# Cross-attention layer with experts: heads weighed by 64-column matmuls, one reciprocal and one product a unit, and the norm of some slots moved to ScalarE

## Chip, core and metric

One core of one Trainium2 chip runs the whole layer in one launch. The metric is the device time in microseconds, the median of several runs.

## The reference, cut to what matters

There are 64 sequences of 64 tokens with 128 features, 16 heads of 8 features, and 8 experts of which each token uses two.

```python
def _attn(q_in, k_in, v_in, wq, bq, wk, bk, wv, bv, wo, bo, causal):
    Q = (q_in @ wq + bq).reshape(Bq, Sq, H, HD)
    Kp = (k_in @ wk + bk).reshape(Bq, Sk, H, HD)
    V = (v_in @ wv + bv).reshape(Bq, Sk, H, HD)
    scores = jnp.einsum('bqhd,bkhd->bhqk', Q, Kp) / jnp.sqrt(jnp.float32(HD))
    if causal:
        scores = jnp.where(mask, scores, -jnp.inf)
    a = jax.nn.softmax(scores, axis=-1)
    o = jnp.einsum('bhqk,bkhd->bqhd', a, V).reshape(Bq, Sq, Dm)
    return o @ wo + bo
...
x = _layernorm(x + _attn(x, x, x, ..., causal=True), ln1_g, ln1_b)
x = _layernorm(x + _attn(x, ctx, ctx, ..., causal=False), ln2_g, ln2_b)
x = _layernorm(x + _moe(x, ...), ln3_g, ln3_b)
```

## The kernel before

The 4096 tokens are 32 tiles of 128 rows, each tile two sequences of 64 tokens. A unit is one attention (self or cross) over one tile, so there are 64 units; two units with consecutive tiles make a block. The program of each engine is written out as a loop over slots. Slot g starts unit g: self blocks first, then two self units and two cross units in turn, then only cross units; the 64 units fill slots 0 to 63. A unit passes through the engines over several slots: scores and maxima in slot g, transposed scores and exponentials in g + 1, weighing and the division by the sum in g + 2, turning the outputs, the output projection, the residual and its statistics in g + 3, the norm and its gain in g + 4, turning the normed rows in g + 5. The projections for later blocks are prepared in the same slots (`prepared`, `crossed`). From slot 33 on, each slot also holds one or more tiles of the experts (88 tiles in all, most of them after the attention), and slots 24 to 26, 40 to 42 and 56 to 58 hold routing steps. Each engine executes its instructions in order and waits on counting semaphores; the order within a slot is that of the functions `slot(g)`.

In a slot, TensorE does, in order: turn outputs and normed rows (`turn_both`; after the scores where `turns_late(g)` holds, that is in slots without tiles before slot 33), transposed scores of unit g - 1 (`scores_T`, which needs VectorE's `max_diag`), scores of unit g (`scores`), an expert tile's first products, router logits, `weigh` of unit g - 2, `out_proj` of unit g - 3, the tile's second products, and projections for later blocks. VectorE does: low parts of the projections (`low_parts`), `norm` of unit g - 4, `maxima` of unit g, the low parts of the first 10 heads' probabilities, logits, `outputs` of unit g - 2 and `residual` of unit g - 3, then routing and sums. ScalarE does the two exponentials of unit g - 1 (full and high half), copies of what TensorE turned, the tile's copies and Gelu, and the high parts of projections. GpSimd does `gain` of unit g - 4 (waits for the norm), scatters of routed rows, the low parts of the other six heads, `spread` of unit g - 3 (the reciprocal root, from VectorE's mean and variance) and the low part of the second norm's output.

`weigh` multiplies the probabilities of a pair of heads (keys on the partitions) with the values in fp16, as three products of high and low parts. Two sequences share a tile. Both halves of the columns, one for each head of the pair, meet values of both heads, so half of the 36 columns of each result are not used: the rows of head h need only the columns of head h. The values hold an extra column of ones per head, whose result is the softmax's denominator. `outputs` divides by it, for each half of the partitions apart, into `o_n`, whose other half was set to zero at the start, so that `turn_o` can sum it over 128 partitions.

Of the kernel before, what the change touches and what calls it, by code (L numbers as in the profile page):

```python
# [7 lines left out]
HD = D // H  # L8
P = 128
# [7 lines left out]
HP = H // 2  # L17
# [367 lines left out]
def build(nc, x, ctx_in, cst, w, out):  # L385
# [17 lines left out]
    with st:  # L403
# [52 lines left out]
        o_n = [sb(f"o_n{p}", [P, 2, 2, HP, HD]) for p in range(2)]  # L456
# [5 lines left out]
        rstd = [sb(f"rstd{p}", [P, 1]) for p in range(2)]  # L462
        carrier = sb("carrier", [P, 1])
# [42 lines left out]
        LG_COL = 36 * HP  # L506
# [66 lines left out]
        zeroed, ZEROED = sem("constants_set"), 22  # L573
# [248 lines left out]
        def _(pool):  # L822
# [6 lines left out]
            for p in range(2):  # L829
                pool.memset(o_n[p][:, :, :, :, :], 0.0).then_inc(zeroed, 1)  # L830
# [4 lines left out]
            pool.wait_ge(zeroed, 14)  # L835
            for a in range(2):
                for p in range(2):
                    for b in range(2):
                        pool.memset(v_hi[a][p][64 * b:64 * b + 64, :, b, :, HD:HD + 1], 1.0).then_inc(zeroed, 1)
                        pool.wait_ge(zeroed, 14 + 4 * a + 2 * p + b + 1)  # L840
# [28 lines left out]
            def spread(u):  # L869

                a, n = u.kind, u.buf
                pool.wait_ge(mv_done[a], u.count())
                pool.tensor_tensor(veps[n][:, :], mv[n][:, 1:2], eps[:, 0:1], ALU.add).then_inc(ve_done[a], 1)  # L873
                pool.wait_ge(ve_done[a], u.count())
                pool.tensor_tensor(rstd[n][:, :], veps[n][:, :], minus_half[:, 0:1], ALU.pow).then_inc(rs_done[a], 1)  # L875

# [57 lines left out]
            def slot(g):  # L934
# [17 lines left out]
                if u := unit_at(g - 3):  # L952
                    spread(u)
# [13 lines left out]
        def _(act):  # L967
# [72 lines left out]

            def x2_high(u):

                act.wait_ge(x_done[CROSS], u.count())
                act.activation(x2_hl[:, u.tile(), 0:D], x_rows[:, u.tile(), :], ACT.Copy).then_inc(x2_hi_ready, 1)
# [48 lines left out]
            def slot(g):  # L1093
# [71 lines left out]
        def _(dve):  # L1165
# [52 lines left out]

            def outputs(u):

                a = u.kind
                dve.wait_ge(pv_ready[a], u.count())
                o = bank[:, O_B, 0:HP * 36].rearrange("p (a b c d) -> p a b c d", a=HP, b=2, c=2)
# [11 lines left out]
            def residual(u):  # L1235
# [10 lines left out]
                dve.wait_ge(res_done[a], u.count())  # L1246
                dve.bn_stats(stats[n][:, :], res[n][:, :]).then_inc(st_done[a], 1)
                dve.wait_ge(st_done[a], u.count())
                dve.tensor_copy(carrier[:, :], consts[:, 0:1])
                dve.bn_aggr(mv[n][:, :], stats[n][:, :]).then_inc(mv_done[a], 1)  # L1250

            def norm(u, v):

                a, n = u.kind, u.buf
                dve.wait_ge(rs_done[a], u.count())
# [202 lines left out]
            def slot(g):  # L1458
# [20 lines left out]
                if u := unit_at(g - 4):  # L1479
                    norm(u, same_buffers(g - 4))  # L1480
# [50 lines left out]
        def _(pe):  # L1531
# [125 lines left out]
            def weigh(u):  # L1657
# [5 lines left out]
                a2, p2 = home(a, b)  # L1663
                for p in range(HP):
                    ph, pl = [v[u.buf][:, 2 * p:2 * p + 2, :].rearrange("p h q -> p (h q)") for v in (p_hi, p_lo)]
                    vh, vl = [v[a2][p2][:, u.pair, :, 2 * p:2 * p + 2, :].rearrange("p b h d -> p b (h d)")
                              for v in (v_hi, v_lo)]
# [266 lines left out]
```

## Time and profile before

| | us |
|---|---|
| median of 3 runs | 741.23 (740.14 to 742.75) |
| profiled execution | 739.34 |
| span of the profiled execution | 737.5 |
| busy in the span: TensorE, weight loads | 566.0, 451.3 |
| busy in the span: VectorE, ScalarE, GpSimd | 493.5, 436.8, 360.7 |

The profile is one execution. The span runs from the first to the last instruction; what lies between span and time is start and end of the launch. Matmuls are pipelined and their ends are modelled, so the starts of consecutive matmuls say more than their durations. In the names of engines PE is TensorE, PEld its weight loads, DVE VectorE, ACT ScalarE, POOL GpSimd. Idle time in square brackets stands before an instruction, with what ended it.

### The profile page before, as it was taken

What the parts mean: (1) busy time and instruction counts of PE and PEld (TensorE: products, weight loads), DVE (VectorE), ACT (ScalarE), POOL (GpSimd) and SP (SyncE); (2) the same over time, 40 slices, a digit from 0 to 9 for tenths busy, and PEclk for the clock granted to TensorE, in tenths of its full rate; (3) what the DMA queues carried; (4) which work ended last, traced back from release to release, by engine and by line L of the source; (5) the groups of instructions that cost most, each with busy time, mean ns of one, the idle gap of its engine ahead of it and who ended that gap; (6) DMA issues with size and microseconds to landing.
All of it is one profiled execution on the core that took longest, in us unless ns stands there. A gap on an engine that the chain in (4) does not pass through costs nothing. (4 is left out here: it accounts for less than half of the span.)

```text
span 737.5 us, 21262 instructions
## 1 busy us (share of the span) xinstructions
PE 566.0 (77%) x7870; PEld 451.3 (61%) x7870; DVE 493.5 (67%) x1345; ACT 436.8 (59%) x814; POOL 360.7 (49%) x564
## 2 busy tenths in 40 slices
PE   2579767877857779887798888857788877788980
PEld 1256545655544557766677666646687877677980
DVE  4388999999997877778777679996632424231163
ACT  1244665555534459997699789956666763444320
POOL 8133435345327734543576356728852574540360
PEclk9997999799987789999899999997999999999995
DMA  4455434645543456454555746434358898898730
GB/s 101 133 175 158 135 108 148 174 150 164 172 125 94 126 162 205 133 162 133 153 175 153 219 151 195 145 97 143 126 164 255 266 292 287 270 282 257 237 105 28
DMA packets 142837, 124.65 MB, mean 169 GB/s; under 512 B 12752, under 2 KB 125152, under 8 KB 142736
## 3 DMA queue, kind: packets, MB, share of 16 engines
q1 hardware_dynamic: 135024, 113.06, 50.5%
q0 software_dynamic: 4176, 8.53, 4.1%
q10 hardware_dynamic: 3536, 1.70, 0.8%
q8 instruction: 64, 1.05, 0.6%
q14 instruction: 37, 0.30, 0.1%
HBM read 86.81 MB, written 38.54 MB: 170 GB/s over the span
## 5 line engine op out<-in xcount | busy, mean ns | idle before, releaser
L1212 DVE TENSOR_REDUCE row_max<-bank 128x16 bf16<-128x1024 f32 x64 | 78.1, 1221 | 32.3 <-PE bank L1627 31.2
L1767 PE MATMUL bank<-w_in,w_hl 128*128 128x128 f32 x704 | 98.8, 284 | 0.0
L1004 ACT ACTIVATE probT<-bank 128x1024 f32<-128x1024 f32 x64 | 65.6, 1024 | 51.2 <-PE bank L1652 50.2
L887 POOL TENSOR_TENSOR prob_lo<-probT,prob_hi 128x384 f16<-128x384 f32 x64 | 66.8, 1044 | 46.9 <-ACT prob_hi L1007 46.5
L1767 PEld LDWEIGHTS bank<-w_in,w_hl 128*128 128x128 f32 x704 | 86.5, 194 | 0.2
L873 POOL TENSOR_TENSOR veps<-mv,eps 128x1 f32<-128x1 f32 x64 | 16.0, 251 | 136.8 <-DVE mv L1250 136.8
L1056 ACT ACTIVATE w_hl<-bank 128x512 f32<-128x512 f32 x88 | 52.6, 598 | 43.5 <-PE bank L1753 42.9
L896 POOL DMA_INDIRECT xs<-x_hl,pos x60 | 63.6, 1060 | 22.8 <-issue 17.2
L1753 PE MATMUL bank<-xT,w_in 128*128 128x128 f16 x1056 | 74.2, 220 | 0.0
L912 POOL DMA_INDIRECT w_hl<-ys,pos x52 | 51.7, 994 | 41.0 <-DMA ys<-w_hl 26.8
L1677 PE MATMUL bank<-consts,o_n 128*128 128x64 f32 x256 | 44.6, 300 | 30.4 <-DVE o_n L1231 26.8
L1640 PE MATMUL bank<-max_diag,consts_bf 128*128 128x512 bf16 x128 | 44.7, 434 | 28.7 <-DVE max_diag L1217 28.6
L1007 ACT ACTIVATE prob_hi<-bank 128x1024 f16<-128x1024 f32 x64 | 65.1, 1018 | 0.0
L1753 PEld LDWEIGHTS bank<-xT,w_in 128*128 128x128 f16 x1056 | 63.8, 99 | 0.0
L1677 PEld LDWEIGHTS bank<-consts,o_n 128*128 128x128 f32 x256 | 36.2, 204 | 44.8 <-issue 30.4
L1652 PEld LDWEIGHTS bank<-q_st,k_all 128*64 128x64 f16 x2048 | 41.9, 121 | 32.5 <-issue 32.5
L1217 DVE TENSOR_TENSOR max_diag<-consts_bf,row_max 128x1024 bf16<-128x1024 bf16 x64 | 59.9, 936 | 2.2
L1205 DVE TENSOR_TENSOR prob_lo<-probT,prob_hi 128x640 f16<-128x640 f32 x64 | 58.3, 910 | 4.0 <-ACT prob_hi L1007 3.9
L861 POOL TENSOR_TENSOR yg<-yn,ln_g 128x128 f32<-128x128 f32 x64 | 29.6, 462 | 56.1 <-DVE yn L1259 56.1
L1749 PE MATMUL bank<-chosen_biases,b_all 128*128 128x128 f16 x352 | 35.1, 222 | 23.0 <-ACT xT L1049 15.0
L1259 DVE TENSOR_SCALAR yn<-res,mv,rstd 128x128 f32<-128x128 f32 x64 | 25.7, 401 | 37.4 <-POOL rstd L875 36.5
L1652 PE MATMUL bank<-q_st,k_all 128*64 128x64 f16 x2048 | 49.3, 207 | 0.0
(182 smaller groups left out, 1536.6 us busy)
## 6 DMA issues: line engine op xcount, KB each, us to landing
w_in<-w_scr SPq DMA_DIRECT2D x96, 512.0 KB, 4.6
q_scr<-q_hl SPq DMA_DIRECT2D x64, 128.0 KB, 2.7
k_scr<-k_hl SPq DMA_DIRECT2D x64, 128.0 KB, 2.3
q_st<-q_scr SPq DMA_DIRECT2D x32, 256.0 KB, 3.1
k_all<-k_scr SPq DMA_DIRECT2D x128, 64.0 KB, 2.5
xs_tile<-xs SPq DMA_DIRECT2D x42, 128.0 KB
ys<-w_hl SPq DMA_DIRECT2D x42, 128.0 KB
xs<-xs_tile SPq DMA_DIRECT2D x19, 256.0 KB, 3.3
```

The source lines that it names most:

```text
L887: pool.tensor_tensor(p_lo[u.buf][:, h, :], probT[u.buf][:, h, :], p_hi[u.buf][:, h, :], ALU.subtract).then_inc(lo_second[u.kind], 1)
L896: pool.indirect_dma_start(xs[c], bass.IndirectOffsetOnAxis(pos[c][:, k, t:t + 1], 0), x2_hl[:, n, :], None).then_inc(scattered[c], 16)
L1004: act.activation(probT[u.buf][:, :, :].rearrange("p h q -> p (h q)"), bank[:, KEYS:KEYS + 2, :].rearrange("p a n -> p (a n)"), ACT.Exp, sc ...
L1007: act.activation(p_hi[u.buf][:, :, :].rearrange("p h q -> p (h q)"), bank[:, KEYS:KEYS + 2, :].rearrange("p a n -> p (a n)"), ACT.Exp, sca ...
L1056: act.activation(hid[x.par][:, :, :].rearrange("p c t -> p (c t)"), expert_h(x), ACT.Gelu, scale=1 / W1_SCALE).then_inc(h_done, 1)
L1205: dve.tensor_tensor(p_lo[u.buf][:, h, :], probT[u.buf][:, h, :], p_hi[u.buf][:, h, :], ALU.subtract).then_inc(lo_first[u.kind], 1)
L1212: dve.reduce_max(row_max[u.buf][:, :], bank[:, SC:SC + 2, :].rearrange("p a (h k) -> p (a h) k", k=S), AX.X).then_inc(max_done[a], 1)
L1217: dve.tensor_tensor(max_diag[u.buf][:, :, :, :], dl, m, ALU.mult).then_inc(diag_ready[a], 1)
L1652: last = pe.matmul(bank[64 * h:64 * h + 64, KEYS + n, 64 * hh:64 * hh + 64], k[:, gg, j, c:c + 64], q[:, gg, c:c + 64], start=False, stop= ...
L1677: last = pe.matmul(turned_o[:, 64 * b:64 * b + 64], o_n[u.buf][:, b, :, :, :].rearrange("p c a d -> p (c a d)"), consts[:, C_DELTA:C_TRI], ...
L1753: last = pe.matmul(v[:, c * P:(c + 1) * P], w1_t[x.wb][:, i, c * P:(c + 1) * P], xT[x.par][:, j * P:(j + 1) * P], start=False, stop=True, ...
L1767: last = pe.matmul(expert_y(x), hid[x.par][:, c, :], w2_t[x.wb][:, c, :], start=False, stop=c == FC - 1, skip_group_check=True)
```

## The change

`weigh` uses each head's probabilities as weights of 64 columns and streams that head's 18 columns of values (both sequences, ones included); the two heads of a pair write to the two halves of the partitions. There are 48 matmuls a unit where there were 24. All 18 columns of each result are used, so `outputs` becomes one reciprocal and one product over 128 partitions, `o_n` has half the size and needs no zeros, and `turn_o` takes four 64 x 64 products for two of 128 x 64. On VectorE the order of a slot's end is now: residual of unit g - 3, reciprocal of unit g - 2, statistics of g - 3, product of g - 2 (in place of a small copy), mean and variance of g - 3. GpSimd makes an offset, -mean x rstd, after the root; both `norm`s wait for it. In slots where `turns_late(g)` holds, ScalarE does the norm of unit g - 4 from scale and offset, behind its copies of the turned rows; elsewhere VectorE does it as before.

```diff
-        o_n = [sb(f"o_n{p}", [P, 2, 2, HP, HD]) for p in range(2)]
+        o_n = [sb(f"o_n{p}", [P, 2, HP, HD]) for p in range(2)]
+        shift = [sb(f"shift{p}", [P, 1]) for p in range(2)]
-        LG_COL = 36 * HP
+        LG_COL = 2 * (HD + 1) * HP
 # GpSimd, start
-            for p in range(2):
-                pool.memset(o_n[p][:, :, :, :, :], 0.0).then_inc(zeroed, 1)
 # GpSimd
-            def spread(u):
+            def spread(u, v):
                 a, n = u.kind, u.buf
                 pool.wait_ge(mv_done[a], u.count())
+                if v:
+                    pool.wait_ge(yn_ready[v.kind], v.count())
                 pool.tensor_tensor(veps[n][:, :], mv[n][:, 1:2], eps[:, 0:1], ALU.add).then_inc(ve_done[a], 1)
                 pool.wait_ge(ve_done[a], u.count())
                 pool.tensor_tensor(rstd[n][:, :], veps[n][:, :], minus_half[:, 0:1], ALU.pow).then_inc(rs_done[a], 1)
+                pool.wait_ge(rs_done[a], 2 * u.count() - 1)
+                pool.tensor_scalar(shift[n][:, :], mv[n][:, 0:1], rstd[n][:, :], -1.0, ALU.mult, ALU.mult).then_inc(rs_done[a], 1)
 # ScalarE
+            def norm(u, v):
+                a, n = u.kind, u.buf
+                act.wait_ge(rs_done[a], 2 * u.count())
+                if u.count() > 1:
+                    act.wait_ge(yn_ready[a], u.count() - 1)
+                if v:
+                    act.wait_ge(yT_ready[v.kind], v.count())
+                    act.wait_ge(yg_done[v.kind], v.count())
+                act.activation(yn[n][:, :], res[n][:, :], ACT.Identity, bias=shift[n][:, :], scale=rstd[n][:, :]).then_inc(yn_ready[a], 1)
...
                 if turns_late(g):
                     both_turned(g)
+                    if u := unit_at(g - 4):
+                        norm(u, same_buffers(g - 4))
 # VectorE
-            def outputs(u):
+            def denominators(u):
                 a = u.kind
                 dve.wait_ge(pv_ready[a], u.count())
-                for h in range(2):
-                    r = slice(64 * h, 64 * h + 64)
-                    last = dve.reciprocal(rden[u.buf][r, :, :], o[r, :, :, h, HD])
-                last.then_inc(rden_done[a], 1)
+                dve.reciprocal(rden[u.buf][:, :, :], weighed()[:, :, :, HD]).then_inc(rden_done[a], 1)
+            def outputs(u):
+                a = u.kind
                 dve.wait_ge(rden_done[a], u.count())
-                for h in range(2):
-                    r = slice(64 * h, 64 * h + 64)
-                    last = dve.tensor_tensor(o_n[u.buf][r, :, h, :, :].rearrange("p b a d -> p a b d"), o[r, :, :, h, 0:HD],
-                                             rden[u.buf][r, :, :].unsqueeze(3).to_broadcast([64, HP, 2, HD]), ALU.mult)
-                last.then_inc(on_ready[a], 1)
+                dve.tensor_tensor(o_n[u.buf][:, :, :, :].rearrange("p b a d -> p a b d"), weighed()[:, :, :, 0:HD],
+                                  rden[u.buf][:, :, :].unsqueeze(3).to_broadcast([P, HP, 2, HD]), ALU.mult).then_inc(on_ready[a], 1)
...
+                if v:
+                    dve.wait_ge(yn_ready[v.kind], v.count())      # in residual(u, v)
...
-                if u := unit_at(g - 4):
+                if (u := unit_at(g - 4)) and not turns_late(g):
                     norm(u, same_buffers(g - 4))
...
-                if u := unit_at(g - 2):
-                    outputs(u)
-                if u := unit_at(g - 3):
-                    residual(u)
+                u, v = unit_at(g - 3), unit_at(g - 2)
+                if u:
+                    residual(u, same_buffers(g - 3))
+                if v:
+                    denominators(v)
+                if u:
+                    row_stats(u)
+                    mean_and_variance(u, v)      # outputs(v) before the aggregate
+                elif v:
+                    outputs(v)
 # TensorE
+                n = 2 * (HD + 1)
                 for p in range(HP):
-                    for k, (pt, v) in enumerate(((ph, vh), (ph, vl), (pl, vh))):
-                        last = pe.matmul(bank[:, O_B, 36 * p:36 * p + 36], pt, v, start=k == 0, stop=k == 2,
-                                         skip_group_check=True)
+                    for k, (pt, v) in enumerate(((p_hi, v_hi), (p_hi, v_lo), (p_lo, v_hi))):
+                        for h in range(2):
+                            last = pe.matmul(bank[64 * h:64 * h + 64, O_B, n * p:n * p + n], pt[u.buf][:, 2 * p + h, :],
+                                             v[a2][p2][:, u.pair, :, 2 * p + h, :], start=k == 0, stop=k == 2,
+                                             skip_group_check=True)
...
                 for b in range(2):
-                    last = pe.matmul(turned_o[:, 64 * b:64 * b + 64],
-                                     o_n[u.buf][:, b, :, :, :].rearrange("p c a d -> p (c a d)"),
-                                     consts[:, C_DELTA:C_TRI], start=True, stop=True)
+                    for h in range(2):
+                        r = slice(64 * h, 64 * h + 64)
+                        last = pe.matmul(turned_o[r, 64 * b:64 * b + 64], o_n[u.buf][r, b, :, :].rearrange("p a d -> p (a d)"),
+                                         consts[r, C_DELTA:C_TRI], start=True, stop=True)
```

## Rows read from the trace of the kernel before

**Rows 1.** Windows: stretch, length, PE, PEld, DVE, ACT, POOL busy, clock, DMA share, GB/s.

```profile
45.00:255.00 210.00, 161.95 (x2321) 112.41 (x2321) 186.75 (x457) 107.26 (x207) 97.97 (x169) 0.87 0.49 146
255.00:530.00 275.00, 226.94 (x3446) 179.93 (x3445) 212.26 (x573) 225.66 (x381) 151.44 (x235) 0.93 0.52 158
```

**Rows 2.** VectorE's groups by form, 45 to 255 us: count, busy, mean ns, idle before.

```profile
L1212 DVE TENSOR_REDUCE row_max<-bank 128x16 bf16<-128x1024 f32 x29 | 35.4, 1219 | 2.8 <-PE bank L1627 2.4
...
L1231 DVE TENSOR_TENSOR o_n<-bank,rden 64x128 f32<-64x128 f32 x57 | 16.5, 289 | 1.4
L1226 DVE RECIPROCAL rden<-bank 64x16 f32<-64x16 f32 x56 | 14.0, 250 | 0.4
...
L1259 DVE TENSOR_SCALAR yn<-res,mv,rstd 128x128 f32<-128x128 f32 x28 | 11.2, 399 | 13.1 <-POOL rstd L875 12.7
...
L1476 DVE SCALAR_TENSOR_TENSOR w_hl<-w_in,w_hl 128x512 f16<-128x512 f32 x8 | 5.3, 665 | 0.0
```

**Rows 3.** TensorE's timeline over four slots: start, duration, line, tiles, count, idle before.

```profile
170.64 0.62 PE L1640 MATMUL bank<-max_diag,consts_bf 128*128 128x512 bf16 x2 [0.84 <-DVE max_diag L1217]
...
177.30 0.62 PE L1640 MATMUL bank<-max_diag,consts_bf 128*128 128x512 bf16 x2 [1.40 <-DVE max_diag L1217]
...
181.18 0.49 PE L1685 MATMUL bank<-wo,oT 128*128 128x128 f32 x2 [0.46 <-ACT oT L1016]
...
181.94 0.61 PE L1607 MATMUL bank<-wv,inT 128*128 128x128 f32 x4
183.50 0.62 PE L1640 MATMUL bank<-max_diag,consts_bf 128*128 128x512 bf16 x2 [0.95 <-DVE max_diag L1217]
...
186.10 0.63 PE L1677 MATMUL bank<-consts,o_n 128*128 128x64 f32 x4 [0.92 <-DVE o_n L1231]
...
187.66 0.36 PE L1704 MATMUL bank<-rw,x_tile 128*128 128x8 f32 x2 [0.81 <-ACT x_tile L1030]
...
189.96 1.06 PE L1607 MATMUL bank<-wv,inT 128*128 128x128 f32 x4
...
197.74 0.62 PE L1640 MATMUL bank<-max_diag,consts_bf 128*128 128x512 bf16 x2 [0.87 <-DVE max_diag L1217]
```

**Rows 4.** TensorE's timeline inside two slots, the parts that are priced.

```profile
173.96 0.18 PE L1669 MATMUL bank<-v_hi,prob_hi 128*128 128x36 f16 x1
...
174.56 0.47 PE L1685 MATMUL bank<-wo,oT 128*128 128x128 f32 x2
...
177.76 0.59 PE L1645 MATMUL bank<-consts_bf 128*128 128x512 bf16 x2
178.28 0.69 PE L1652 MATMUL bank<-q_st,k_all 128*64 128x64 f16 x32
178.81 0.61 PE L1627 MATMUL bank<-k_all,q_st 128*64 128x256 f16 x8
179.34 0.66 PE L1677 MATMUL bank<-consts,o_n 128*128 128x64 f32 x4
179.84 0.28 PE L1690 MATMUL bank<-consts,yn 128*128 128x128 f32 x1
```

**Rows 5.** ScalarE's groups by form, the whole span.

```profile
L1025 ACT ACTIVATE x1T<-bank,ln_bc,ln_gc 128x128 f32<-128x128 f32 x32 | 14.8, 463 | 0.0
```

**Rows 6.** GpSimd's groups by form, 45 to 255 us.

```profile
L896 POOL DMA_INDIRECT xs<-x_hl,pos x12 | 13.5, 1124 | 3.6 <-issue 3.6
...
L873 POOL TENSOR_TENSOR veps<-mv,eps 128x1 f32<-128x1 f32 x28 | 8.8, 314 | 80.1 <-DVE mv L1250 80.1
```

**Rows 7.** TensorE's timeline in a slot with scatters.

```profile
245.00 0.18 PE L1669 MATMUL bank<-v_hi,prob_hi 128*128 128x36 f16 x1 [1.78 <-POOL prob_lo L887]
```

**Rows 8.** Waits from 255 to 530 us: total, times, longest.

```profile
DVE row_max L1212 <- PE bank L1627: 24.9, 14, 4.6
...
ACT oT L1016 <- PE bank L1690: 19.3, 14, 3.1
```

**Rows 9.** GpSimd's timeline at the start.

```profile
8.35 0.60 POOL L830 MEMSET o_n<- 128x256 f32 x2
```

More of the change, by code:

```diff
@@ L572, in build @@
         cbf_ready = sem("consts_bf16_ready")
-        zeroed, ZEROED = sem("constants_set"), 22
+        zeroed, ZEROED = sem("constants_set"), 20
         b1_bo_ready = sem("ln1_b_plus_ca_bo")
@@ L834, in _ @@
             pool.memset(b_all[:, :], 0.0).then_inc(zeroed, 1)
-            pool.wait_ge(zeroed, 14)
+            pool.wait_ge(zeroed, 12)
             for a in range(2):
@@ L839, in _ @@
                         pool.memset(v_hi[a][p][64 * b:64 * b + 64, :, b, :, HD:HD + 1], 1.0).then_inc(zeroed, 1)
-                        pool.wait_ge(zeroed, 14 + 4 * a + 2 * p + b + 1)
+                        pool.wait_ge(zeroed, 12 + 4 * a + 2 * p + b + 1)
             for dst, src in [(v[:, :], w[name].partition_broadcast(P)) for v, name in (
@@ L952, in slot @@
                 if u := unit_at(g - 3):
-                    spread(u)
+                    spread(u, same_buffers(g - 3))
                 if (u := unit_at(g - 6)) and u.kind == CROSS:
@@ L1217, in maxima, with weighed, residual @@
                 dve.tensor_tensor(max_diag[u.buf][:, :, :, :], dl, m, ALU.mult).then_inc(diag_ready[a], 1)
+            def weighed():
+                return bank[:, O_B, 0:LG_COL].rearrange("p (a b d) -> p a b d", a=HP, b=2)
+            def denominators(u):
+                a = u.kind
+                dve.wait_ge(pv_ready[a], u.count())
+                dve.reciprocal(rden[u.buf][:, :, :], weighed()[:, :, :, HD]).then_inc(rden_done[a], 1)
             def outputs(u):
                 a = u.kind
-                dve.wait_ge(pv_ready[a], u.count())
-                o = bank[:, O_B, 0:HP * 36].rearrange("p (a b c d) -> p a b c d", a=HP, b=2, c=2)
-                for h in range(2):
-                    r = slice(64 * h, 64 * h + 64)
-                    last = dve.reciprocal(rden[u.buf][r, :, :], o[r, :, :, h, HD])
-                last.then_inc(rden_done[a], 1)
-                dve.wait_ge(rden_done[a], u.count())
-                for h in range(2):
-                    r = slice(64 * h, 64 * h + 64)
-                    last = dve.tensor_tensor(o_n[u.buf][r, :, h, :, :].rearrange("p b a d -> p a b d"), o[r, :, :, h, 0:HD],
-                                             rden[u.buf][r, :, :].unsqueeze(3).to_broadcast([64, HP, 2, HD]), ALU.mult)
-                last.then_inc(on_ready[a], 1)
-            def residual(u):
+                dve.wait_ge(rden_done[a], u.count())
+                dve.tensor_tensor(o_n[u.buf][:, :, :, :].rearrange("p b a d -> p a b d"), weighed()[:, :, :, 0:HD],
+                                  rden[u.buf][:, :, :].unsqueeze(3).to_broadcast([P, HP, 2, HD]), ALU.mult).then_inc(on_ready[a], 1)
+            def residual(u, v):
                 a, n = u.kind, u.buf
                 dve.wait_ge(wo_ready[a], u.count())
+                if v:
+                    dve.wait_ge(yn_ready[v.kind], v.count())
                 if a == SELF:
@@ L1245, in residual, with row_stats, mean_and_variance @@
                 dve.tensor_tensor(res[n][:, :], bank[:, O_B, WO_COL:WO_COL + D], r, ALU.add).then_inc(res_done[a], 1)
[L1246 to L1250, printed above, removed]
+            def row_stats(u):
+                dve.wait_ge(res_done[u.kind], u.count())
+                dve.bn_stats(stats[u.buf][:, :], res[u.buf][:, :]).then_inc(st_done[u.kind], 1)
+            def mean_and_variance(u, v):
+                dve.wait_ge(st_done[u.kind], u.count())
+                if v:
+                    outputs(v)
+                else:
+                    dve.tensor_copy(carrier[:, :], consts[:, 0:1])
+                dve.bn_aggr(mv[u.buf][:, :], stats[u.buf][:, :]).then_inc(mv_done[u.kind], 1)
             def norm(u, v):
                 a, n = u.kind, u.buf
-                dve.wait_ge(rs_done[a], u.count())
+                dve.wait_ge(rs_done[a], 2 * u.count())
+                if u.count() > 1:
+                    dve.wait_ge(yn_ready[a], u.count() - 1)
                 if v:
@@ L1491, in slot @@
                     logits(u)
-                if u := unit_at(g - 2):
-                    outputs(u)
-                if u := unit_at(g - 3):
-                    residual(u)
+                u, v = unit_at(g - 3), unit_at(g - 2)
+                if u:
+                    residual(u, same_buffers(g - 3))
+                if v:
+                    denominators(v)
[3 more added lines that the diff above has]
+                elif v:
+                    outputs(v)
                 if (c := routed_at(g, 2)) is not None:
```

3 lines of the change are left out of this document (removed).

## The prediction

> **What bounds the kernel now.** I read the windows first [rows 1]. From 45 to 255 us the kernel runs the slots that have attention but no expert tiles. VectorE is busy 186.75 of 210 us there, TensorE (modelled, overlapping) 161.95, ScalarE 107.26, GpSimd 97.97. From 255 to 530 us, where every slot also has expert tiles, TensorE (226.94 of 275) and ScalarE (225.66) lead and VectorE has 212.26. After 530 us only tiles and the last expert pass remain; the chain that ended last lies in that part and is TensorE's, so what is gained or lost before 530 us shifts it as a whole.
>
> Then VectorE's groups of the first stretch [rows 2]: 29 maxima, so 29 slots. Outside its own work VectorE sat idle mainly before the norm: 13.1 us, 12.7 of it until GpSimd's rstd came. Then TensorE's order over four slots [rows 3], 170.64 to 197.74 us, the repeating pattern: two self units, two cross units, 27.10 us, 6.78 a slot. Each slot begins with the product that needs VectorE's max_diag, and TensorE waited 1.40, 0.95 and 0.87 us for it in three of the four, and 0.92 us for o_n in one. So VectorE sets the pace there, with TensorE and ScalarE close behind. That closeness decides the forecast.
>
> **VectorE, slots without tiles.** Removed a slot: the norm, 0.40 us, and the wait before it, 12.7 / 28 = 0.45 us [rows 2]; one reciprocal of two (0.25) and one product of two (0.29), because the new ones cover 128 partitions with as many elements per partition (16 and 128) as each half had [rows 2]. A one-element copy goes too; it overlaps and I count nothing. Sum 1.39 us a slot, which would leave 5.39. The new order, residual, reciprocal, statistics, product, aggregate, has the product waiting on a reciprocal with another instruction between, so nothing is queued behind a fresh dependence. The heads' product is the fourth instruction after the start, as before, so on_ready does not come earlier; the aggregate has four instructions in front of it instead of seven, so it comes 0.54 us earlier.
>
> **TensorE, every unit.** Weighing: 24 matmuls of 36 columns take 174.56 - 173.96 = 0.60 us, 25 ns each [rows 4]. The new 48 have 64-column weights and 18 columns to stream. The nearest row is the scores' transposed product, also 64-column weights alternating between the two partition halves: 32 in 178.81 - 178.28 = 0.53 us, 16.6 ns each [rows 4]. 48 x 16.6 = 0.80 us. Entering such weights costs something: 178.28 - 177.76 = 0.52 us for two products of 512 columns, whose repeat without a change of shape (177.30 to 177.76, two) took 0.46 [rows 3, 4]; 0.06 in, and I take as much out. The weighing thus rises by 0.80 + 0.12 - 0.60 = 0.32 us. Lower bound 0 (half the columns per weight load, so half the time for each), upper bound 48 x 25 ns + 0.12 - 0.60 = +0.72.
>
> Turning the outputs: two fp32 products (four records) take 179.84 - 179.34 = 0.50 us [rows 4]; four of 64 x 64 take eight records. No row shows fp32 on a quarter of the array. Lower bound -0.10 (the halves overlap wholly), upper bound 8 x 0.125 + 0.1 = 1.1, so +0.60. I take +0.15, nearer the low end, because the 16.6 ns row shows the two halves overlapping.
>
> The page TensorEngine Tiling (Array Packing) of the Trainium skill, section Instruction Overhead, says each matmul has about 60 cycles of overhead however few columns it streams, and its section Key Properties says that a change of tiling mode drains the engine. Counted per instruction the first would make 48 matmuls 1.2 us; the row of 16.6 ns speaks against that for alternating halves, and the 0.06 us agrees with a small drain. By that page the weighing would rise 0.60 us, 0.28 more than I take, and over the 15 steady slots of the sum below 4.2 us of gain would go: 727 instead of 723.
>
> **What becomes the bound there.** TensorE's period without its waits for max_diag is 27.10 - 1.40 - 0.95 - 0.87 = 23.88 us. I leave the 0.92 us for o_n in: later in that slot TensorE waits 0.81 us for ScalarE's x_tile anyway [rows 3]. Added: weighing 0.32 in each of three slots, turn 0.15 in one; in the second slot both together are 0.47, which the 0.46 us wait for oT [rows 3] hides; in the last two the turn hides in the x_tile wait. 3 x 0.32 + 0.15 = 1.11, so 24.99. In one slot the four products of V took 1.06 us against 0.61 for the same in the slot before [rows 3], and the granted clock over the stretch was 0.87 [rows 1]: TensorE had waited for o_n and x_tile, then ran for a while at the lower of its two levels (1.2 and 2.4 GHz). Those products lost 0.45; with the projections beside them I estimate 1.0 us for the slot, and with fewer waits I give back half, 0.5. Period 24.5, 6.12 a slot: 0.66 gained, out of VectorE's 1.39.
>
> **ScalarE and GpSimd.** ScalarE's norm is the form of its y copy, 128 x 128 with a scale and an offset per row: 0.46 us [rows 5]. It stands behind two exps and both turned copies. ScalarE is busy half of this stretch [rows 1], so 29 x 0.46 fits, but the norm is in order: behind it wait the copies of projections, then the next exps. It needs rstd and the offset one slot after the aggregate, and the aggregate now comes earlier. GpSimd's offset is one 128 x 1 operation that multiplies twice: between the add beside it, 0.31 us [rows 6], and two of them, 0.62; I take 0.31, and either is hidden under its 80.1 us of waiting for mv in this stretch [rows 6]. What moves for GpSimd is its gain: it waits for ScalarE's norm, late in the slot, and the low parts of the probabilities are queued behind the gain. The weighing that needs them is a slot later, so about 1 us of room; free. In slots with tiles VectorE's norm waits for the offset too, +0.31, against an aggregate 0.54 earlier: nothing.
>
> The four slots with scatters (twelve of 1.12 us [rows 6]) are GpSimd's already: TensorE waited 1.78 us for its low parts [rows 7]. No gain there.
>
> **Slots with tiles.** Here VectorE loses 0.54 us a slot, but it is not the pace: it waits 24.9 us for scores, and ScalarE waits 19.3 us in 14 slots for the turned y, right behind the turned outputs [rows 8]. 14 x 0.15 = 2.1 us lost. Four slots hold VectorE's routing steps and gain 0.54 each, 2.2. The weighing's 0.32 stands ahead of the down products, which wait for ScalarE's tile copies often enough that I take it as hidden; exposed in half of 32 slots it costs 5.1 us. Net 0.
>
> **Start.** Two memsets of o_n go, 8.35 us, 0.60 for both [rows 9], ahead of GpSimd's loads: 0.5 us.
>
> **Sum.** 29 slots: 4 with scatters 0; 8 where VectorE also splits W1 (0.67 each, [rows 2]) and 2 with routing, where more of the 1.39 is usable: 1.0 each, 10.0; the other 15 at 0.66, 9.9. Less 0.1 in each of 25 slots, because in slots that split projections VectorE itself will be late for the scores: 2.5. 10.0 + 9.9 - 2.5 + 0.5 = 17.9. From the profiled execution's 739.34 us: 721.4. The median of the runs shown, 741.23, is 1.9 above; so 723.
>
> **Rivals.** *VectorE stays the pace*: TensorE overlaps the halves wholly and its clock rises with fewer waits. Then 25 slots gain 1.39: 34.8 us, 706. For it: VectorE's 89% busy. Against: 23.88 of 27.10.
>
> *TensorE too slow*: the small matmuls cost 25 ns each, as the row of the old weighing has it, and the eight records do not overlap: +0.72 + 0.60 = 1.32 a unit. A steady slot becomes 23.88 / 4 + 1.32 = 7.29, 0.51 slower than now; 15 slots give 8 us, the 14 waits for the turn 8 more, and the ten others nothing: slower, about 757. It decides from 6.78 - 5.97 = 0.81 us a unit on. Against: the 16.6 ns row. The page's overhead of the Trainium skill named above is this rival's first half.
>
> *GpSimd and ScalarE in line*: the gain behind ScalarE's norm pushes the low parts beyond the weighing, as GpSimd already does in the scatter slots [rows 7]. At 0.35 us a slot over 25 slots half the gain goes: 732. Against: about 1 us of room.
>
> *Nothing*: ScalarE's order alone (exps, copies, norm, projections) fills 6.78 us a slot: 741. Against: it is half idle.
>
> **Chances.** Forecast 0.55, VectorE the pace 0.15, GpSimd in line 0.15, nothing 0.05, TensorE too slow 0.10. The forecast by itself runs from 715 (full 1.39 in the ten slots, VectorE never late, clock all given back) to 730 (weighing exposed in half the tile slots, no clock back). The range reaches to 706 and, past 732, to 739. About 0.3%, 2.2 us, is what a measurement can tell from no change. Faster 0.82, same 0.06, slower 0.12.
>
> **What would show it.** Right: plain slots without tiles near 6.1 us; VectorE's wait for rstd gone and its waits for the scores grown; TensorE's waits for max_diag small; weighing near 0.92 us, the turn near 0.65; slots with scatters and with tiles as they are. Wrong: the weighing waiting for GpSimd's low parts in plain slots; the turned outputs over 1.0 us; TensorE's clock in the first stretch lower than 0.87; tile slots longer than now.

## The result, and the profile after

The kernel after takes 722.4 us (median of four runs, 720.5 to 724.3) against 741.4 for the kernel before on the same chip: a ratio of 0.974 with a 95% interval from 0.971 to 0.978. Medians here are over all runs of a kernel, and ratios leave out the runs of a slower state that some executions fall into. The forecast was 723. The profiled execution took 722.76 us with a span of 720.9. The total came out as predicted; its parts did not, as the slots show. I cut both traces, one execution of each kernel, at the starts of the 64 maxima, one a slot:

| stretch | before, us | after, us | gained | by the prediction's terms |
|---|---|---|---|---|
| up to the maxima of slot 3 | 46.11 | 46.58 | -0.5 | 0.5 |
| slots 3 to 14, no router logits yet | 88.12 | 72.83 | 15.3 | 9.4 |
| slots 15 to 23, router logits in five of the nine | 61.00 | 61.02 | 0.0 | 5.0 |
| slots 24 to 32, scatters and routing among them | 75.40 | 73.52 | 1.9 | 2.9 |
| slots 33 to 60, with tiles | 242.28 | 240.12 | 2.2 | 0 |
| the rest of the span | 224.59 | 226.83 | -2.2 | 0 |

The column of the prediction's terms takes 0.9 for each of the 8 slots that split W1 (7 to 14) and of the 2 with routing, and 0.56 for each steady slot, that is its 1.0 and 0.66 less the 0.1 for lateness.

The windows of the kernel after, for [rows 1]; columns as there. The second and the third cut the first stretch as the table does:

```profile
45.00:245.00 200.00, 171.72 (x3222) 120.59 (x3215) 153.75 (x356) 121.79 (x244) 117.10 (x200) 0.86 0.56 165
...
46.58:119.41 72.83, 64.28 (x1319) 44.20 (x1319) 63.13 (x135) 52.34 (x102) 43.66 (x74) 0.95 0.58 172
119.41:180.43 61.02, 54.93 (x982) 39.37 (x982) 43.21 (x96) 34.66 (x74) 32.63 (x60) 0.80 0.57 167
```

VectorE, 89% busy in [rows 1], is at 77% now. In slots 3 to 14 the granted clock (TensorE's clock as a share of its full 2.4 GHz) is 0.95 and the twelve slots take 83% of their time before; in slots 15 to 23 the clock is 0.80, and VectorE is idle for 29% of them. VectorE's groups, for [rows 2]:

```profile
L1228 DVE TENSOR_REDUCE row_max<-bank 128x16 bf16<-128x1024 f32 x30 | 36.7, 1224 | 21.1 <-PE bank L1662 20.6
...
L1248 DVE TENSOR_TENSOR o_n<-bank,rden 128x128 f32<-128x128 f32 x29 | 8.4, 291 | 1.0
...
L1242 DVE RECIPROCAL rden<-bank 128x16 f32<-128x16 f32 x29 | 7.1, 245 | 0.0
```

One product of 291 ns and one reciprocal of 245 ns stand where there were two each, and the norm with its wait for rstd is gone. In their place VectorE waits 20.6 us for TensorE's scores. TensorE's order in slot 19, the second of two cross units, and in slot 21, for [rows 3, 4]:

```profile
144.68 0.45 PE L1714 MATMUL bank<-consts,o_n 64*64 64x64 f32 x8
145.06 0.33 PE L1726 MATMUL bank<-consts,yn 128*128 128x128 f32 x1
147.03 0.36 PE L1740 MATMUL bank<-rw,x_tile 128*128 128x8 f32 x2 [1.64 <-ACT x_tile L1033]
147.32 0.23 PE L1703 MATMUL bank<-v_hi,prob_hi 128*64 128x18 f16 x2
...
148.71 0.80 PE L1721 MATMUL bank<-wo,oT 128*128 128x128 f32 x2
149.29 1.06 PE L1638 MATMUL bank<-inT,wk 128*128 128x256 f32 x2
150.15 1.06 PE L1642 MATMUL bank<-wv,inT 128*128 128x128 f32 x4
...
162.90 0.20 PE L1703 MATMUL bank<-v_hi,prob_hi 128*64 128x18 f16 x2
...
163.76 0.49 PE L1721 MATMUL bank<-wo,oT 128*128 128x128 f32 x2
164.09 0.60 PE L1638 MATMUL bank<-inT,wq 128*128 128x256 f32 x2
```

The weighing takes 163.76 - 162.90 = 0.86 us at the full clock (0.92 were forecast), and the turn 145.06 - 144.68 = 0.38 (0.65 were forecast, 0.50 was before). But TensorE stands still for 1.64 us in front of the router logits, which need ScalarE's x_tile (the turned rows of unit g - 5, which the router's weights multiply); then everything takes longer. The weighing behind the wait lasts 148.71 - 147.32 = 1.39 us and the projections 1.06 where others take 0.60. The windows of slots 19, 20 and 21 show the granted clock beside it:

```profile
145.73:154.70 8.97, 7.67 (x106) 5.45 (x108) 5.29 (x13) 4.56 (x10) 3.62 (x7) 0.62 0.67 195
154.70:162.38 7.68, 6.87 (x115) 4.48 (x117) 4.05 (x10) 3.29 (x9) 3.73 (x7) 0.78 0.48 137
162.38:167.11 4.73, 4.73 (x110) 3.44 (x112) 4.58 (x11) 3.02 (x7) 2.76 (x5) 1.00 0.46 151
```

And the waits from 45 to 245 us (total, times, longest):

```profile
POOL yg L860 <- ACT yn L1053: 50.4, 27, 4.4
...
DVE row_max L1228 <- PE bank L1662: 20.6, 13, 3.3
...
PE bank L1740 <- ACT x_tile L1033: 11.5, 9, 2.1
...
ACT yn L1053 <- POOL shift L878: 7.4, 3, 3.8
...
PE bank L1675 <- DVE max_diag L1233: 3.4, 3, 1.7
```

TensorE waits 3.4 us for max_diag; before it was three waits in four slots [rows 3]. The largest of its waits is now that for x_tile. Theory A was therefore: in slots 15 to 23 the wait for x_tile and the lower clock behind it took the gain. Its rivals: ScalarE's chain with the norm in it sets these slots (B, C), and in the slots with scatters GpSimd and ScalarE stand in line, as the prediction's third rival had it.

### The profile page after: what moved, and what is told of

Read it like the earlier page. It is cut to its first block and busy times, and to the rows that moved or that the text cites. A ratio compares the mean times of both kernels' runs of the same rounds, so it can differ in the third digit from the quotient of the medians.

```text
span 720.9 us, 24904 instructions
## 1 busy us (share of the span) xinstructions
PE 584.9 (81%) x9662; PEld 466.0 (65%) x9662; DVE 418.1 (58%) x1125; ACT 447.0 (62%) x843; POOL 386.3 (54%) x626
## 3 DMA queue, kind: packets, MB, share of 16 engines
q8 instruction: 78, 1.28, 0.7%
## 5 line engine op out<-in xcount | busy, mean ns | idle before, releaser
L1803 PE MATMUL bank<-w_in,w_hl 128*128 128x128 f32 x704 | 100.5, 288 | 0.0
L1803 PEld LDWEIGHTS bank<-w_in,w_hl 128*128 128x128 f32 x704 | 88.2, 197 | 0.3
L860 POOL TENSOR_TENSOR yg<-yn,ln_g 128x128 f32<-128x128 f32 x64 | 32.7, 511 | 94.6 <-ACT yn L1053 54.7
L1010 ACT ACTIVATE prob_hi<-bank 128x1024 f16<-128x1024 f32 x64 | 65.2, 1019 | 0.0
L1703 PE MATMUL bank<-v_hi,prob_hi 128*64 128x18 f16 x1024 | 58.9, 183 | 6.2 <-issue 3.9
L1221 DVE TENSOR_TENSOR prob_lo<-probT,prob_hi 128x640 f16<-128x640 f32 x64 | 61.8, 965 | 3.3 <-ACT prob_hi L1010 3.3
L1703 PEld LDWEIGHTS bank<-v_hi,prob_hi 128*64 128x64 f16 x1024 | 53.0, 117 | 10.5 <-issue 6.9
L1703 PE MATMUL bank<-v_hi,prob_lo 128*64 128x18 f16 x1024 | 57.8, 180 | 0.0
L1703 PE MATMUL bank<-v_lo,prob_hi 128*64 128x18 f16 x1024 | 57.8, 180 | 0.0
L1703 PEld LDWEIGHTS bank<-v_hi,prob_lo 128*64 128x64 f16 x1024 | 53.6, 118 | 0.0
L1703 PEld LDWEIGHTS bank<-v_lo,prob_hi 128*64 128x64 f16 x1024 | 53.4, 117 | 0.0
L1785 PE MATMUL bank<-chosen_biases,b_all 128*128 128x128 f16 x352 | 35.4, 223 | 20.6 <-ACT xT L1063 12.3
```

The source lines that it names most:

```text
L1010: act.activation(p_hi[u.buf][:, :, :].rearrange("p h q -> p (h q)"), bank[:, KEYS:KEYS + 2, :].rearrange("p a n -> p (a n)"), ACT.Exp, sca ...
L1221: dve.tensor_tensor(p_lo[u.buf][:, h, :], probT[u.buf][:, h, :], p_hi[u.buf][:, h, :], ALU.subtract).then_inc(lo_first[u.kind], 1)
L1703: last = pe.matmul(bank[64 * h:64 * h + 64, O_B, n * p:n * p + n], pt[u.buf][:, 2 * p + h, :], v[a2][p2][:, u.pair, :, 2 * p + h, :], star ...
L1785: pe.matmul(v[:, c * P:(c + 1) * P], b_all[:, c * P:(c + 1) * P], sel[x.c][:, 0, x.k:x.k + 1].to_broadcast([P, P]), start=c == 0, stop=Tru ...
L1803: last = pe.matmul(expert_y(x), hid[x.par][:, c, :], w2_t[x.wb][:, c, :], start=False, stop=c == FC - 1, skip_group_check=True)
```

## The experiments

"Steady period" is the time of slots 19 to 22: 27.10 us before, 26.95 after, 24.5 by the prediction.

**The logits moved behind the weighing.**

```diff
-                if v and v.kind == CROSS:
+                if v and v.kind == CROSS and not turns_late(g):
                     logits(v)
                 if u:
                     weigh(u)
                 if u := unit_at(g - 3):
                     out_proj(u)
+                if v and v.kind == CROSS and turns_late(g):
+                    logits(v)
```

> The kernel after with one move on TensorE: in slots without tiles the router logits, which wait for ScalarE's x_tile, stand behind the weighing and the output projection instead of ahead of them. Theory A (the steady slots 15 to 24 gained nothing because TensorE stands in line for x_tile, 1.2 to 2.1 us in each second slot, and then runs at the lower clock): the wait shrinks to under 0.5 us since 1.2 us of work moves into it, the granted clock of slots 15 to 24 rises, and the four-slot period falls from 26.95 to about 24.5: 715 us. Rival B (ScalarE's chain of exponentials, copies, norm and projections sets the steady slots, and TensorE's wait is only where that shows): the wait turns up elsewhere in the slot and the time stays within 2 us of 722.

> The same kernel as the one with the logits behind the weighing, timed again beside the two others of this call: 713 us by its first timing (710.9 to 717.2). The steady period again near 21 us, at a granted clock of 1.00 in slots 19 to 24; where single slots fall to the lower clock may differ from the first time.

Measured: 713.1 us both times; ratios to the kernel before 0.965 [0.958, 0.972] and 0.964 [0.960, 0.967], the second one wholly below that of the kernel after. The steady period fell to 20.87 and 21.28 us, further than expected. Window of the first one's slots 19 to 22, and its TensorE where the wait was:

```profile
147.53:168.40 20.87, 20.24 (x462) 14.76 (x462) 18.18 (x43) 15.80 (x33) 14.33 (x26) 1.00 0.66 193
```
```profile
167.73 0.33 PE L1726 MATMUL bank<-consts,yn 128*128 128x128 f32 x1
169.27 0.49 PE L1721 MATMUL bank<-wo,oT 128*128 128x128 f32 x2 [0.34 <-ACT oT L1019]
169.61 0.39 PE L1740 MATMUL bank<-rw,x_tile 128*128 128x8 f32 x2
```

The weighing fills the wait, and TensorE is busy for 20.24 of 20.87 us at a clock of 1.00. Theory A holds, and rival B falls.

**The wait filled with products that nobody reads**, to part the clock from the wait.

```diff
+            def idle_work(n):
+                for _ in range(n):
+                    pe.matmul(bank[:, H_B, :], ident_bf, mask_key..., start=True, stop=True)
...
                 if v and v.kind == CROSS:
+                    if turns_late(g):
+                        idle_work(7 if unit_at(g).kind == CROSS and unit_at(g - 1).kind == CROSS else 4)
                     logits(v)
```

> The kernel after with work added: in slots without tiles TensorE runs four or seven products of 128 x 512 that nobody reads ahead of the router logits, about as long as the wait for x_tile there. It tests the clock alone: the wait is filled, not removed. Theory A's second half (the clock that falls behind the wait costs the steady slots their gain): granted clock 1.00 in slots 15 to 24 where it was 0.59 to 0.78 in five of ten; at full clock such a slot is 1.0 to 1.5 us shorter, so 5 to 7 us are gained: 716 us. Rival B (ScalarE's chain sets the steady slots): the clock rises and the time does not fall by more than 2 us. If the wait is of use to nobody but the products overrun it in slots 3 to 14, some 0.5 us a slot is lost there: up to 727 us.

Measured: 717.1 us (713.0 to 721.3), 0.972 [0.965, 0.978]. By the time alone that can't be told from the kernel after; the slots tell. Window of slots 19 to 22, and of slots 19 and 20:

```profile
144.10:167.53 23.43, 22.30 (x449) 15.44 (x448) 18.73 (x42) 15.70 (x33) 14.80 (x28) 1.00 0.65 190
...
144.10:150.35 6.25, 6.21 (x117) 4.08 (x116) 5.29 (x12) 3.93 (x10) 3.47 (x7) 1.00 0.71 199
150.35:156.65 6.30, 5.93 (x113) 3.79 (x112) 3.79 (x9) 3.83 (x10) 3.77 (x7) 1.00 0.52 164
```

With the same logits in the same place, mainly the clock differs: 26.95 - 23.43 = 3.5 us a period were the clock's. The other 23.43 - 20.87 = 2.6 us were the wait's. In slots 19 and 20 alone, which hold the logits, the clock's part is 16.65 - 12.55 = 4.1 us and the wait's 12.55 - 10.35 = 2.2; in the other two slots the filled kernel is 0.6 us slower, as TensorE stands still there for 0.72 us in front of a new block's scores (see the last section).

**The two parts one by one.** The first kernel leaves out ScalarE's `norm` and GpSimd's `shift`, and VectorE norms everywhere; the second adds only these two to the kernel before.

```diff
-                    if u := unit_at(g - 4):                        # ScalarE, first kernel
-                        norm(u, same_buffers(g - 4))
...
-                if (u := unit_at(g - 4)) and not turns_late(g):    # VectorE, first kernel
+                if u := unit_at(g - 4):
                     norm(u, same_buffers(g - 4))
```

> The kernel after without one part: no norm on ScalarE and no offset from GpSimd, VectorE norms in every slot. The weighing, the one reciprocal and product and the new order of VectorE stay. By the prediction's terms VectorE is then relieved of 0.54 us a slot, not 1.39, and of a part of the wait for rstd by the earlier aggregate (0.54): 0.6 to 1.0 in each of the 25 slots without scatters where it is the pace, less TensorE's 0.32: 731 us. Theory A (TensorE's wait and clock cap the steady slots at 6.75 whatever VectorE is relieved of): slots 15 to 24 as in the kernel after, only slots 3 to 14 gain less: about 728. Rival C (the norm in ScalarE's order costs the steady slots, and GpSimd's gain behind it the scatter slots): the scatter slots 27, 29 and 31 win back up to 7 us, and the time comes to 720 or less.

> The kernel before with the other part alone: ScalarE norms in slots without tiles from GpSimd's offset, and the old weighing, the two reciprocals and products and the old order of VectorE stay. By the prediction's terms 0.40 + 0.45 us a slot go from VectorE, and TensorE has nothing added: 0.85 in 12 slots and 0.66 in 15 steady ones at most, 730 us; if the two parts simply add up, this one and the weighing alone come to the whole change's 19 us. Rival C (the norm on ScalarE is bad for slots 15 to 32): gains in slots 3 to 14 of 8 to 10 us, nothing in 15 to 24, and the same loss in slots 27 to 32 as the whole change showed: 735 us.

Measured: 723.0 us (716.5 to 729.0; 0.980 [0.973, 0.988]) and 725.7 (0.980 [0.973, 0.986]). By the ratios each part alone is worth about three quarters of the whole change. Windows of slots 19 to 22, without and with ScalarE's norm alone:

```profile
145.88:172.87 26.99, 24.34 (x436) 17.15 (x436) 21.01 (x46) 14.18 (x28) 12.06 (x23) 0.81 0.57 168
```
```profile
151.25:175.76 24.51, 21.02 (x326) 14.80 (x326) 23.63 (x55) 15.97 (x32) 15.38 (x28) 0.93 0.63 186
```

Without any norm on ScalarE the steady period is the same 27.0 at the same clock of 0.81, so ScalarE's norm is not what cost these four slots: rival C falls there. In slots 15 to 18 it is otherwise: they took 22.97 us at a clock of 1.00 without ScalarE's norm, where the kernel after took 26.31 (and 24.94 in the run with the scatters moved below, which has the same code there), although TensorE waits 1.51 and 1.28 us for x_tile without that norm too. Theory A had these slots unchanged; whether the norm or chance set the clock there, one trace does not tell. With the old weighing VectorE still fills 23.63 of 24.51 us, TensorE waits 0.59 us for max_diag, 0.46 for o_n and 0.84 and 0.99 for x_tile, and the norm alone does bring 2.6 us a period.

**The same square with the logits behind.** The move of the first experiment on the kernel before, and on each of the two kernels with one part.

> The kernel before with one move: logits behind the weighing and the output projection in slots without tiles, nothing of the change. The prediction's view (VectorE sets the pace of those slots before the change; TensorE's wait of 0.8 to 1.0 us for x_tile hides in VectorE's time): steady period 27.1 to 26.5, total 738 to 741 us. Rival (the wait for x_tile and the clock behind it were the bound before the change already, and the change's gain in slots 3 to 14 came from elsewhere): the period falls to 24 or less and the time to 725 or less, nearly as the whole change.

> The kernel after without ScalarE's norm and GpSimd's offset (VectorE norms everywhere), and with the logits behind the weighing and the output projection. It shows what the norm on ScalarE is worth once the wait for x_tile is out of the way. Theory A: with the wait gone VectorE sets the pace again, so that its 0.40 us norm and its wait for rstd count in full: steady period 20.9 + 4 x 0.4 to 0.85 = 22.5 to 24.3, total 717 to 720 us against 713. Rival (ScalarE is the next bound, so that a norm taken from it is worth as much as the one given to VectorE costs): period 21 or less, 713 or less.

> The kernel before with ScalarE's norm and GpSimd's offset, and with the logits behind the weighing and the output projection; the old weighing, both reciprocals and products and the old order of VectorE stay. It is the fourth corner of a square whose others are: neither part (740.3), the weighing's part alone (716.9), both parts (713.1), all with the logits behind. Theory A (VectorE is the pace of slots 3 to 24 until both parts are in, and each microsecond taken from it counts): the norm's part takes 0.85 us a slot in 21 slots, 722 us; the steady period 23.5 to 24.5, as with the logits ahead (24.5), since VectorE and not TensorE ends the slot. Rival (the new order of VectorE's queue is what counted, not the time taken from it): 730 us or more.

| median, us (ratio to before) | logits ahead | logits behind |
|---|---|---|
| neither part | 741.4 | 740.3 (0.9985 [0.9953, 1.0017]) |
| weighing's part | 723.0 (0.980) | 716.9 (0.965 [0.959, 0.971]) |
| norm's part | 725.7 (0.980) | 726.1 (0.983 [0.979, 0.987]) |
| both | 722.4 (0.974) | 713.1 (0.964 [0.960, 0.967]) |

On the kernel before, the move is worth nothing, as the prediction's view of VectorE wants it; with the norm's part alone nothing either (steady period 24.50 and 24.51). Only where the weighing's part has relieved VectorE do the logits stand in the way. Once they are out of it, ScalarE's norm costs the steady slots nothing: without it the period is 23.83 us, with it 20.87 and 21.28. With them behind, the norm's part is worth 3.8 us on top of the weighing's by the medians (the intervals overlap), and the two do not add up (23.4 and 14.2 alone, 27.2 together), since TensorE becomes the pace.

**The slots with scatters.** First GpSimd's scatters behind its other work, alone and with the logits moved:

```diff
-                for c, n, k in scatters_at(g):
-                    scatter(c, n, k)
+                if not turns_late(g):                  # GpSimd, as before
+                    for c, n, k in scatters_at(g):
+                        scatter(c, n, k)
...
                 if (u := unit_at(g - 6)) and u.kind == CROSS:
                     x2_low(u)
+                if turns_late(g):
+                    for c, n, k in scatters_at(g):
+                        scatter(c, n, k)
```

> The kernel after with one move on GpSimd: in slots without tiles its three scatters (1.12 us each, in slots 25, 27, 29 and 31) stand behind the low parts of the probabilities, the root, the offset and the low part of the second norm, instead of ahead of them. Theory (GpSimd and ScalarE stand in line in these four slots: TensorE's weighing waits 1.6 and 0.7 us for prob_lo, ScalarE's norm 7.4 us in three waits for shift): these waits go, slots 25 to 32 fall from 67.2 us to about 63, total 718 us. Rival (those slots are set by the wait for x_tile and the clock, as the steady ones; GpSimd's lateness is hidden in it): 67.2 stays within 1 us. Against a gain: the routed rows are written later, so the first expert tile (slot 33) may wait for its rows; that could give back 1 to 3 us in slot 32.

> The kernel after with both moves: logits behind the weighing and the output projection, and GpSimd's scatters behind its other work in the slot. If the two causes are separate, the gains add: slots 15 to 24 as with the logits moved alone (51 us in place of 61), slots 25 to 32 below the 65.2 us of that kernel, about 61; total 709 us. If the scatters' place does not matter (rival), 713 as with the logits moved alone.

Measured: 720.0 us (0.973 [0.966, 0.979]) and 716.7 (705.7 to 723.5; 0.959 [0.950, 0.969]). Slots 25 to 32 took 66.2 us instead of 67.2 in the first; the second's times spread too far for a reading. Then VectorE's norm from slot 25 on, and products that nobody reads ahead of the weighing, both on top of the moved logits:

```diff
-                    if u := unit_at(g - 4):                          # ScalarE
+                    if (u := unit_at(g - 4)) and g < 25:
                         norm(u, same_buffers(g - 4))
```
```diff
                 if u:
+                    if turns_late(g) and g >= 28:
+                        idle_work(7)
                     weigh(u)
```

> The kernel with the logits behind the weighing, with one more edit: from slot 25 on VectorE norms again, as in the slots with tiles, so that ScalarE's norm stays in slots 4 to 24 alone. Theory (in the slots with scatters GpSimd and ScalarE stand in line: ScalarE's norm waits 8.6 us in three for GpSimd's shift, GpSimd's gain 11.8 us in six for ScalarE's norm, TensorE 6.2 us in three for prob_lo behind it): slots 25 to 32 fall from 65.2 us to the 63.8 of the kernel without any norm on ScalarE, and the waits of the weighing there from 6.2 to about 4.8; total 711 to 712 us. Rival (VectorE becomes late there and the products wait for max_diag instead): 65 us or more, 713 us or more.

> The kernel with the logits behind the weighing, with work added: in the slots without tiles from 28 to 32 TensorE runs seven products of 128 x 512 that nobody reads ahead of the weighing, where it waits 2.5, 2.1 and 1.6 us for GpSimd's prob_lo. It asks what sets those last slots (29 to 32: 8.9, 9.4, 8.5 and 7.5 to 9.3 us at a granted clock of 0.64 to 0.82 and 1.00). Theory A (the clock behind the waits, as in the steady slots): granted clock near 1.00, slots 28 to 32 fall from 39.4 to 41.2 us to about 34; total 707 us. Theory C (GpSimd's line of scatters, low parts and gain sets them): the clock rises, the weighing still waits for prob_lo or begins at the same time after the maximum, the time stays within 2 us of 713; the added products can lose 0.5 us where prob_lo is early.

Measured: 714.8 us (0.966 [0.962, 0.969]), with 65.9 us for slots 25 to 32 against 65.2 and 63.4 in the two runs with ScalarE's norm there: no gain. And 716.3 (0.967 [0.963, 0.972]). Windows of slots 28 to 32 with the logits moved (second run; the first took 41.16 us), and with the products added:

```profile
206.12:245.47 39.35, 31.78 (x560) 22.11 (x561) 25.75 (x52) 20.09 (x44) 29.64 (x47) 0.83 0.45 135
```
```profile
206.08:247.84 41.76, 37.12 (x595) 23.84 (x596) 23.61 (x52) 19.87 (x43) 28.14 (x45) 0.89 0.48 145
```

The clock rose from 0.83 to 0.89 and the time did not fall; even behind the added products the weighing of slot 31 still stood 2.66 us. That wait ended 0.10 us after GpSimd's prob_lo, which had itself stood behind three scatters. By this the clock alone does not set these slots. ScalarE's norm waits up to 3.8 us for GpSimd's shift there, and TensorE for prob_lo, so the line exists; but neither of the two ways out of it that were tried gains over 1 us, and what sets those slots stays open.

## Why the prediction was right in its total

*VectorE as the pace before, and what was taken from it*: right. Reciprocal, product, norm and the wait for rstd went as priced. The square shows it best: the moved logits do nothing for the kernel before.

*TensorE's additions*: right, slightly high, 0.86 for 0.92 and 0.38 for 0.65. By 48 matmuls in 0.86 us one took 17.9 ns, near the row of 16.6 that was taken, and not the 25 of the old weighing. By an estimate from the about 60 cycles of overhead a matmul that the Trainium skill's page TensorEngine Tiling (Array Packing), section Instruction Overhead, states, they would have taken 1.2 us at 2.4 GHz; these rows do not agree. The rival *TensorE too slow* falls.

*Slots 3 to 14*: too small, 9.4 for 15.3. The step that failed is "the other 15 at 0.66": the TensorE bound was read from a pattern with router logits in two slots of four and used for slots that have none yet (they come five slots behind their cross unit, first in slot 15). Without them there is no wait for x_tile, the clock stays at 0.95, and 1.27 a slot of VectorE's 1.39 came out. Part of the 15.3 is luck: six more of the traces run the same code in these slots, and the seven took 72.8 to 79.1 us, in the median 77.1, gains of 15.3 to 9.0. The difference is mostly in slots 5 and 6 (10.8 to 16.9 us), where TensorE stood for up to 2.1 us in front of a new block's scores (see the last section).

*Slots 15 to 23*: too large, 5.0 for 0.0. The failing term is the clock's: "I estimate 1.0 us for the slot, and with fewer waits I give back half, 0.5". The waits other than those for max_diag did fall, from 0.46, 0.92 and 0.81 [rows 3] and one more of 0.88, together 3.1 us a period, to 1.64 and 0.81; but one of them had grown, and the lower level lasted through two slots of four. It cost 3.5 us a period where 0.5 was charged. Without it the period of 23.43 is near 24.5 less 0.5. That two errors of opposite sign, +5.9 and -5.0, nearly cancelled is why the total was right, and that was luck. How the gain splits also changes with the execution: in the kernel with the scatters moved, whose code is the same up to slot 24, these two stretches gained 10.1 and 1.3.

*VectorE stays the pace*: its price of 1.39 a slot was reached nearly in slots 3 to 14 of this trace (0.75 to 1.27 over the seven), and nowhere behind them. *GpSimd and ScalarE in line*: not in plain slots; GpSimd waits 50.4 us for ScalarE's norm, but TensorE's weighing waits for it only where scatters are.

*Slots with tiles*: right, about nothing. The tile slots 34 to 37 went from 30.51 to 30.18 us; the weighing's added time stayed hidden, and the 2.2 us gained were given back by the span's end. *Start*: 0.5 forecast, and the first maximum did begin 0.7 us earlier (29.80 for 30.54); but 0.5 was lost up to slot 3 in this execution, in which slot 0 took 6.03 us. In the kernel with the scatters moved slot 0 took 4.83, as before, and slot 3 began 0.9 earlier than before.

## What to carry to other kernels

When the pace-setting engine is relieved, look in the next engine's order for the first instruction that waits on a third engine and for what stands behind it without need: here moving two small products behind 1.2 us of ready work was worth 9 us, half as much as the change itself, and nothing at all before the change. A bound read from one pattern of slots holds for slots of that pattern alone. A wait of TensorE is to be priced with the clock behind it, and the price taken from a run in which the wait is filled with idle products. A relieved engine can also overtake the transfers that feed it, as the last section shows. And a gain split by stretches from one trace carries that execution's luck.

## What had not been expected of the hardware

*The clock's price.* Slots 19 and 20, with a wait of 1.64 us and one of 0.81, took 16.65 us; with the waits filled they took 12.55: 4.1 us, more than the waits. Why the lower level (1.2 of 2.4 GHz) lasted through two slots here, and through one before the change, is not settled. The length of a wait does not tell it: in the kernel without ScalarE's norm the waits of 1.51 and 1.28 us in slots 15 and 16 left the clock at 1.00, and those of 0.92 and 0.81 in slots 19 and 20 came with 0.56 and 0.78.

*Waits that the profile does not name.* With the new weighing TensorE stops at times in front of the scores, and the profile names nothing that it waits for. With the logits moved (first run):

```profile
140.33 0.63 PE L1662 MATMUL bank<-k_all,q_st 128*64 128x256 f16 x8 [2.31 <-issue]
...
173.61 0.59 PE L1656 MATMUL bank<-consts_bf 128*128 128x512 bf16 x2 [1.55 <-issue]
...
186.78 1.06 PE L1662 MATMUL bank<-k_all,q_st 128*64 128x256 f16 x8 [2.59 <-issue]
```

In its second run and in the kernel with products ahead of the weighing they stand at the same three places (1.6 to 2.7 us), beside some elsewhere; in the kernel before, and in the one with the norm's part and the logits moved, none over 0.4 us lies between 45 and 250 us. All nine stand in front of the scores of a block's first unit, where the program waits for the block's queries and keys to come back from memory (`q_back`, `k_back`). Where the trace has the landing of the keys, in six of the nine, the wait ends 0.09 us after the last of their four transfers landed. That transfer for the first line above, issued at 137.04 us:

```profile
L688 SPq DMA_DIRECT2D k_all<-k_scr x1: 432/432/432, 137.0 to 137.0; - x1
...
DMA to landing us min/median/max: 3.2/3.2/3.2
```

It landed at 140.24 us and TensorE went on at 140.33. For the other three, at the second line's place, the trace has no landing; the last transfer was issued 2.9 to 3.4 us before the wait ended, so the same cause is likely there but not shown. The waits of 1.5 to 2.1 us in slot 5, in four of the seven traces named above, also end 0.09 us after the keys land. Such a wait costs more than its length: in the first run slots 17 and 18, with the wait of 2.31 us, took 13.77 us, and slots 21 and 22, with the same work, 10.52. So once the logits are out of the way, the next thing in TensorE's way is the transfer of a new block's keys; no run moved these transfers forward.

The loading of TensorE's code would be another suspect. The DMA queues of the page, the kernel before and then after (packets, MB, share):

```profile
q8 instruction: 64, 1.05, 0.6%
```
```profile
q8 instruction: 78, 1.28, 0.7%
```

The queue moved 14 packets more for 24904 - 21262 = 3642 instructions more, about 260 instructions each, and each of the nine waits ends 2.6 to 3.8 us after such a packet starts. But most packets are followed by no wait, the kernel without ScalarE's norm moved 78 too and has no unnamed wait over 0.4 us there, and the landings above leave nothing for the code to explain in the six waits. The Trainium skill's page Runtime: NRT & Kernel Launch, section Instruction fetch mechanics, has code come in blocks of 256 instructions, which agrees with the 260, at a cost that is mostly hidden; no run here shows that cost.
